# Row maxima of two tiles taken by one VectorE instruction where their banks are neighbours

## Chip, core and metric

One core of one Trainium2 chip. The metric is device time of one execution in microseconds; the change is judged by the median of several executions against that of the kernel before.

## What is computed

A batch of eight images of 32x32 positions and 192 channels goes through an attention block and then a Fourier mixing block, each behind a group normalisation and with a residual:

```python
x = x + attention(group_norm(x), w_qkv, w_o)      # 12 heads of 16, 1024 tokens
x = x + fourier(group_norm(x), w1, b1, w2, b2, bias_w, bias_b)
# attention, per image and head:
attn = softmax((q @ k.T) * 16 ** -0.5)            # 1024 x 1024
out  = (attn @ v) @ w_o
# fourier, per image: y = irfft2(mix2(relu(mix1(rfft2(x))))) + x @ bias_w.T + bias_b
```

All in 32-bit floats. The softmax needs, for each head and query, the largest score over 1024 keys; the change concerns how that maximum is taken.

## The kernel before

**Bodies and steps.** The work is a pipeline over the eight images: `body(b)` is run for b = 0 to 7, the middle ones in a hardware loop, and has 48 steps (`IN_BODY`), 16 for each of three groups of four heads. A step makes four score tiles of 128 keys by 512 queries (`score_tile`, L1196) into three banks of the on-chip accumulator memory (`scores`), ScalarE takes exponentials of them (`exponentials`, L889), and TensorE multiplies the four tiles of the step before with the values (`pv`, L1249).

**The maxima.** The exponentials need the row maxima first. Eleven steps ahead (`AHEAD`), `max_tile` (L1228) makes the same scores once more, the other way round, 128 queries by 512 keys, four tiles i = 0 to 3 a step: tiles 0 and 1 are the odd and even head of a pair over the first 512 keys, tiles 2 and 3 over the second. VectorE's `take_max` (L986) reduces each to one column of `row_max` and counts `max_taken` up. After eight steps `full_max` joins the two halves of the keys (L993), TensorE turns it (`turn_shift`, L1236), VectorE splits it (L999, L1002), and SyncE sends it by four transfers into two rows of `q_stack` (`shifts`).

**The ring.** The tiles of the maxima share four banks (`ring`, `RING` = 4) with all other products, the pieces of the normalisation, projection and Fourier stages: prep pieces (turn, mean, var, qk, v) of the next image, post pieces (proj, turn, mean, var, spread, dftw, dfth, lin, mix1, mix2, idfth, idftw) of the one before. `PREP_AT` and `POST_AT` say at which step a piece stands, ahead of tile 0 (`START`) or behind the output products (`MID`). `ring_order` writes entries one after another, 268 a body, and an entry's bank is its number modulo 4 (`RING_NO`). Before it writes an entry, TensorE waits until the entry that last held the bank has been read (`bank_free`, `bank_held`): the one four before it, or, where a body leaves pieces out, the last that was made in this bank. Body 0 has no post pieces, only four small set-up stages in the places of proj; body 7 has no prep pieces.

**TensorE's order in a step** is fixed by hand: START pieces, tile 0, score 0, tile 1, score 1, the output products, MID pieces, score 2, tile 2, score 3, tile 3. VectorE takes the START pieces, tiles 0 and 1, the MID pieces, tiles 2 and 3.

**Facts of the ring order that the prediction uses.** In 74 of the 96 pairs (tiles 0 and 1, tiles 2 and 3) of a body the two banks are neighbours, in 22 the first is bank 3 and the second bank 0. An entry whose bank was held by the first tile of such a neighbouring pair, with nothing but tile 3 and pieces between: tile 1 of a step, held by tile 2 of the step before, at 21 steps, with one START piece between (lin at 1 and 29, turn 2 and 13, proj 8, 9 and 10, qk 16, 18, 21 and 23, var 20, dftw 25 and 26, dfth 31 and 33, mix1 39, mix2 41 and 42, v 44 and 45); tile 0, held likewise, at 9 steps, with two between (5: idftw, turn; 11: var, proj; 14: turned, turn; 17: qk, qk; 22: turned, qk; 28: qk, lin; 35: mix1, mix1; 37: qk, mix1; 47: idfth, idfth). "turned" is the product of `turn_shift`. In the start-up the tiles of the last 11 steps of the order are made without the pieces; there the banks of the pairs run 23, 30, 23, 12, 01, 30, 23, 01, 30, 12, 01, 30, 23, 12, 01, 23, 12, 30, 23, 23, 23, 01.

Of the kernel before, what the change touches and what calls it, by code (L numbers as in the profile page):

```python
# [8 lines left out]
ALU = mybir.AluOpType  # L9
ACT = mybir.ActivationFunctionType  # L10
AX = mybir.AxisListType
F32 = mybir.dt.float32
# [5 lines left out]
NT = TOK // P  # L18
# [4 lines left out]
STEPS = 16  # L23
# [10 lines left out]
TILES = GH * STEPS  # L34
VW = HD + 2
HMAX = GH * NT // 2
TURN_AT = 4
HUNITS = STEPS // 2
SCORE_BANKS, RING = 3, 4
AHEAD = STEPS // 2 + 3  # L40
# [84 lines left out]
IN_BODY = NG * STEPS  # L125
# [47 lines left out]
RING_NO = {entry: n for n, entry in enumerate(RING_ORDER)}  # L173
# [71 lines left out]
def build(nc, consts, x, w_qkv, w_o, w1, b1, w2, b2, bias_w, bias_b, out):  # L245
# [3 lines left out]
    with ctx:  # L249
        def sb(name, shape, dt=F32):  # L250
            return ctx.enter_context(nc.sbuf_tensor(name, shape, dt))

        def bank(name, n=1):
            return ctx.enter_context(nc.psum_tensor(name, [P, n, HALF], F32))

        def sem(name):
            return ctx.enter_context(nc.semaphore(name))
# [29 lines left out]
        row_max = sb("row_max", [P, 2, HMAX])  # L287
        full_max = sb("full_max", [P, HMAX])
        shift = sb("shift", [HMAX, 2, P], F32R)
# [40 lines left out]
        ring = bank("ring", RING)  # L330
# [29 lines left out]
        max_made = sem("max_made")  # L360
        max_taken = sem("max_taken")
# [19 lines left out]
        def after(eng, s, count):  # L381

            if not isinstance(count, int) or count > 0:
                eng.wait_ge(s, count)
# [54 lines left out]
        def ring_bank(entry):  # L439
            return ring[:, RING_NO[entry] % RING, :]  # L440
# [55 lines left out]
        def max_unit(unit, i):  # L496

            half, m = divmod(unit, HUNITS)
            hp, qt = divmod(m, NT // 2)
            return half, hp, qt, 1 - i % 2, i // 2  # L500

        def max_bank(g, unit, i):

            return ring_bank(("max", (STEPS * g + unit - AHEAD) % IN_BODY, i))

        def turned_in(b, u):
            return ring_bank(("turned", u))[0:HMAX, 0:P]
# [1 line left out]
        def halves(b, g, half):  # L509

            return 2 * NG * b + 2 * g + half
# [51 lines left out]
        def _(sp):  # L563
# [34 lines left out]
            def shifts(b, g, half):  # L598
                after(sp, shift_split, 2 * halves(b, g, half) + 2)
                for n, odd in itertools.product(range(2), range(2)):  # L600
                    row = 64 * odd + KQ + n
                    sp.dma_start(q_stack[row:row + 1, g, half, :, :].bitcast(F32),
                                 shift[HMAX // 2 * odd:HMAX // 2 * (odd + 1), n, :].bitcast(F32)
                                 ).then_inc(shift_in, 16)

            def sums_down(slot):
# [65 lines left out]
            def prologue():  # L672
# [30 lines left out]
                for g in range(NG):  # L703
                    for part_of in ("q0", "k", "q1"):
                        stack(0, g, part_of)
                    if g == 1:
                        shifts(0, 0, 0)

            def body(b, prep, post):
                first = isinstance(b, int) and b == 0  # L710
                for u in range(IN_BODY):
# [21 lines left out]
                    if u in shift_steps(prep):  # L733
                        shifts(*next_half(b, u))
# [242 lines left out]
        def _(dve):  # L977
            def take_max(slot, g, unit, i):
                half, hp, qt, odd, which = max_unit(unit, i)
                no = 4 * unit + i  # L980
                m = HMAX // 2 * odd + NT // 2 * hp + qt
                dve.wait_ge(max_made, TILES * slot + no + 1)
                if unit % HUNITS == 0 and i == 0:

                    after(dve, max_joined, 2 * slot + half)
                nc.vector.tensor_reduce(row_max[:, which, m:m + 1],  # L986
                                        max_bank(g, unit, i),
                                        AX.X, ALU.max).then_inc(max_taken, 1)
                if unit % HUNITS == HUNITS - 1 and i == 3:

                    dve.wait_ge(max_taken, TILES * slot + no + 1)
                    after(dve, shift_turned, 2 * slot + half)
                    nc.vector.tensor_tensor(full_max[:, :], row_max[:, 0, :], row_max[:, 1, :],  # L993
                                            ALU.max).then_inc(max_joined, 1)
# [122 lines left out]
            def prologue():  # L1117
                nc.vector.memset(k_stack[:, :, :].bitcast(F32), 1.0).then_inc(stack_ones, 1)
                nc.vector.memset(xt1[CH:CH + 1, 0, :], 1.0).then_inc(ones_set, 1)
                nc.vector.memset(spec_a[CH:CH + 1, :], 1.0).then_inc(ones_set, 1)  # L1120
                for u in range(IN_BODY):
                    for kind, k in in_order({u: PREP_AT.get(u, NO_PIECES)}):
                        prep_piece(0, kind, k, early_bank(PREP_NO[kind, k]))
                    for kind, k in PREP_FOLLOW.get(u, []):
                        follow(0, 0, kind, k)
                for unit in range(AHEAD):
                    for i in range(4):
                        take_max(0, 0, unit, i)
                    if unit == HUNITS:
                        split_shift(0, 0, 0, turned_in(0, IN_BODY - 3))  # L1130

            def body(b, prep, post):
                first = isinstance(b, int) and b == 0
                for u in range(IN_BODY):
# [7 lines left out]
                    for tile in tiles[:2]:  # L1142
                        take_max(tile[0], *tile[2:])
# [4 lines left out]
                    for tile in tiles[2:]:  # L1148
                        take_max(tile[0], *tile[2:])
# [34 lines left out]
        def _(pe):  # L1184
# [33 lines left out]
            def max_tile(body, u, slot, b, g, unit, i):  # L1218
                half, hp, qt, odd, which = max_unit(unit, i)
                no = 4 * unit + i  # L1220
                if unit == 0 and i == 0:
                    pe.wait_ge(stacked[g], STACK_INCS * (b + 1))
                if unit == HUNITS and i == 0:
                    pe.wait_ge(stacked_second[g], SECOND_INCS * (b + 1))

                bank_free(body, ("max", u, i))
                rows = slice(64 * odd, 64 * odd + KQ)
                mm(max_bank(g, unit, i),  # L1228
                   q_stack[rows, g, half, hp, P * qt:P * (qt + 1)],
                   k_stack[rows, 2 * g + hp, HALF * which:HALF * (which + 1)],  # L1230
                   start=True, stop=True).then_inc(max_made, 1)
# [326 lines left out]
```

## Time and profile before

| | us |
|---|---|
| median of 3 runs | 1567.48 (1566.85 to 1567.92) |
| the profiled execution | 1570.3 |
| its span, first to last instruction | 1568.5 |
| TensorE busy | 1490.9 |
| VectorE busy, of it row maxima | 1221.5, 970.3 |
| ScalarE busy | 1005.6 |

The profile is of one execution. Its page gives, for each engine, the time in which instructions are drawn, and then a chain of waits: from the last instruction back, at each point to what released it. TensorE overlaps instructions, so its busy time is no measure of how full it is. Row groups name the instruction, its result and its operand by the kernel's own names, with the line of the kernel before.

### The profile page before, as it was taken

How to read it: one execution, taken by the hardware profiler on the slowest of the kernel's cores; microseconds unless marked ns; L12 is line 12 of the kernel's file. 1: busy time of each engine (PE TensorE's matmuls, PEld its weight loads, DVE VectorE, ACT ScalarE, POOL GpSimd, SP SyncE). 2: the span in 40 equal slices, each digit the busy share in tenths (PEclk: the TensorE clock that was granted, in tenths of full speed). 3: DMA queues.
4: the chain of work that ended last, by engine and by line, in shares of the span. 5: the costliest groups of instructions: out<-in, count | busy, mean ns of one | idle time of the engine just before them, and what ended most of it. 6: DMA issues, size and time to landing. Idle time of an engine off the chain costs nothing.

```text
span 1568.5 us, 28858 instructions
## 1 busy us (share of the span) xinstructions
PE 1490.9 (95%) x8768; PEld 692.1 (44%) x8768; DVE 1221.5 (78%) x2175; ACT 1005.6 (64%) x1945; POOL 166.8 (11%) x257
## 2 busy tenths in 40 slices
PE   7799999999999999999999999999999999999886
PEld 5333334444444444444444453444544444433454
DVE  4888879987798868988599877988699877887031
ACT  2167766777667666767567776777767776767511
POOL 2000001200003000120013000030002100030000
PEclk9599999999999999999999999999999999989999
DMA  5420223143253232333250431532331432411223
GB/s 116 79 50 18 34 49 69 30 74 59 44 110 51 49 75 55 68 69 64 52 110 15 79 70 24 110 52 48 78 72 28 68 68 44 89 28 31 43 48 83
DMA packets 93892, 94.14 MB, mean 60 GB/s; under 512 B 23201, under 2 KB 75170, under 8 KB 93730
## 3 DMA queue, kind: packets, MB, share of 16 engines
q1 hardware_dynamic: 93730, 92.14, 30.0%
q8 instruction: 82, 1.34, 0.4%
q14 instruction: 80, 0.66, 0.1%
HBM read 14.23 MB, written 6.29 MB: 13 GB/s over the span
## 4 chain that ended last, share of the span: by engine, by line
PE 74%; DVE 13%; issue 4%; SPq 3%; DMA 2%; POOL 1%; ACT 1%; DVEq 0%; POOLq 0%
PE o_acc L1249 20%; PE scores L1196 14%; PE ring L1228 13%; DVE row_max L986 10%; PE ring L1272 6%; PE ring L1318 4%; PE ring L1285 2%; PE ring L1385 2%; PE ring L1372 2%; PE ring L1378 2%; PE ring L1294 1%; PE ring L1364 1%; PE ring L1391 1%; PE ring L1260 1%; SPq L628 1%
## 5 line engine op out<-in xcount | busy, mean ns | idle before, releaser
L986 DVE TENSOR_REDUCE row_max<-ring 128x1 f32<-128x512 f32 x1536 | 970.3, 681 | 165.1 <-PE ring L1228 162.3
L889 ACT ACTIVATE probs<-scores 128x512 f32<-128x512 f32 x1536 | 828.7, 598 | 297.8 <-PE scores L1196 292.2
L1228 PE MATMUL ring<-k_stack,q_stack 48*128 48x512 f32 x1536 | 577.2, 461 | 20.6 <-DVE row_max L986 18.1
L1196 PE MATMUL scores<-q_stack,k_stack 50*128 50x512 f32 x1536 | 578.5, 456 | 3.6 <-DMA q_stack<-shift 2.2
L1249 PE MATMUL o_acc<-probs,v_aug 128*18 128x512 f32 x3072 | 409.9, 606 | 2.3 <-ACT probs L889 1.2
L1196 PEld LDWEIGHTS scores<-q_stack,k_stack 50*128 50x128 f32 x1536 | 239.3, 186 | 297.7 <-ACT probs L889 265.2
L1228 PEld LDWEIGHTS ring<-k_stack,q_stack 48*128 48x128 f32 x1536 | 241.0, 189 | 150.6 <-DVE row_max L986 84.6
L545 POOL TENSOR_TENSOR inv_all<-o_raw,inv_all 128x1024 f32<-128x1024 f32 x23 | 54.2, 2357 | 646.2 <-DVE inv_all L1013 646.2
L1249 PEld LDWEIGHTS o_acc<-probs,v_aug 128*18 128x18 f32 x3072 | 51.8, 96 | 128.1 <-issue 87.8
L1318 PE MATMUL ring<-xt,w_qk 96*128 96x256 f32 x336 | 91.8, 399 | 2.3 <-DVE row_max L986 2.2
L1318 PEld LDWEIGHTS ring<-xt,w_qk 96*128 96x128 f32 x336 | 57.6, 189 | 34.0 <-DVE row_max L986 20.9
L1070 DVE TENSOR_TENSOR x<-ring,x 128x384 f32<-128x384 f32 x28 | 15.5, 554 | 52.0 <-PE ring L1285 52.0
L1051 DVE TENSOR_TENSOR qk_parts<-ring,qk_parts 128x256 fp32r<-128x256 f32 x84 | 34.7, 417 | 21.1 <-ACT qk_parts L919 20.4
L919 ACT CAST qk_parts<-ring 128x256 fp32r<-128x256 f32 x84 | 31.3, 372 | 30.5 <-PE ring L1318 29.7
L1272 PE MATMUL ring<-wo,o_t 96*128 96x192 f32 x248 | 48.1, 338 | 0.9 <-DVE tok_n L1082 0.9
L905 ACT COPY xt<-ring 96x512 f32<-96x512 f32 x28 | 16.2, 582 | 45.8 <-PE ring L1260 45.8
L934 ACT COPY rows_a<-ring 128x384 f32<-128x384 f32 x62 | 29.8, 481 | 23.9 <-PE ring L1391 18.0
L1272 PEld LDWEIGHTS ring<-wo,o_t 96*128 96x128 f32 x248 | 39.6, 190 | 10.2 <-DVE row_max L986 4.5
L1285 PE MATMUL ring<-bias_t,xt 97*128 97x192 f32 x224 | 44.0, 339 | 0.0
L1272 PE MATMUL ring<-wv,xt 96*128 96x192 f32 x224 | 43.9, 339 | 0.0
L1025 DVE BATCH_NORM_STATS2 stats<-xt 96x6 f32<-96x512 f32 x64 | 42.9, 678 | 0.5 <-ACT xt L929 0.5
L1272 PEld LDWEIGHTS ring<-wv,xt 96*128 96x128 f32 x224 | 35.6, 189 | 17.0 <-DVE row_max L986 12.3
(163 smaller groups left out, 1039.8 us busy)
## 6 DMA issues: line engine op xcount, KB each, us to landing
q_stack<-qk_parts SPq DMA_DIRECT2D x288, 64.0 KB, 2.8
k_stack<-qk_parts SPq DMA_DIRECT2D x144, 128.0 KB, 4.4
rows_b<-rows_a SPq DMA_DIRECT2D x128, 96.0 KB, 3.0
spec_b<-spec_a SPq DMA_DIRECT2D x64, 102.0 KB, 2.3
x_in<-in_x_dram SPq DMA_DIRECT2D x8, 768.0 KB, 6.5
x_res<-in_x_dram SPq DMA_DIRECT2D x8, 768.0 KB, 6.8
o_t<-inv_all SPq DMA_DIRECT2D x96, 64.0 KB, 2.3
rows_b<-spec_b SPq DMA_DIRECT2D x32, 192.0 KB, 3.2
```

Source lines behind the costliest of these rows:

```text
L545: ops.tensor_tensor(inv_all[:, :], o_raw[:, :], inv_all[:, :], ALU.mult).then_inc(o_normed, 1)
L889: nc.scalar.activation(probs[:, GH * (s % 2) + h, :], scores[:, n % SCORE_BANKS, :], ACT.Exp, scale=SCALE).then_inc(probs_made, 1)
L986: nc.vector.tensor_reduce(row_max[:, which, m:m + 1], max_bank(g, unit, i), AX.X, ALU.max).then_inc(max_taken, 1)
L1025: nc.vector.bn_stats(stats[:, which, c, half, :], what[0:CH, c, HALF * half:HALF * (half + 1)]).then_inc(stats_done[which], 1)
L1051: nc.vector.tensor_tensor(qk_parts[:, 1, k // 4, cols], bank_[:, 0:QUARTER], qk_parts[:, 0, k // 4, cols].bitcast(F32), ALU.subtract).then ...
L1196: mm(scores[:, n % SCORE_BANKS, :], k_stack[rows, 2 * g + hp, P * kt:P * (kt + 1)], q_stack[rows, g, half, hp, :], start=True, stop=True). ...
L1228: mm(max_bank(g, unit, i), q_stack[rows, g, half, hp, P * qt:P * (qt + 1)], k_stack[rows, 2 * g + hp, HALF * which:HALF * (which + 1)], st ...
L1249: last = mm(o_acc[32 * h:32 * h + VW, 0, :], v_aug[:, g, kt, h, :], probs[:, GH * (s % 2) + h, :], start=(kt == 0), stop=(kt == NT - 1), s ...
L1272: last = mm(bank_[:, C * n:C * (n + 1)], lhs[:, c, P * t:P * (t + 1)], rhs[:, c, :], start=(n == 0 and c == 0), stop=(c == 1), skip_group_ ...
L1285: last = mm(bank_[:, C * n:C * (n + 1)], xt1[rows, c, P * t:P * (t + 1)], bias_t[rows, c, :], start=(n == 0 and c == 0), stop=(c == 1), sk ...
L1318: last = mm(bank_[:, 0:QUARTER], w_qk[:, c, P * (k // 4):P * (k // 4 + 1)], xt[:, c, QUARTER * (k % 4):QUARTER * (k % 4 + 1)], start=(c == ...
L1372: last = mm(bank_[0:CH, P * n:P * n + f.shape[1]], rows_b[:, j, CH * chunk:CH * (chunk + 1)], f, start=True, stop=True)
```

## The change

`take_max` compares the bank numbers of tiles i and i | 1. Where the second is the first plus one, tile 0 (or 2) waits for both tiles, and one `tensor_reduce` over two banks, 2 x 512 elements, gives two columns of `row_max` and counts `max_taken` up by two; tile 1 (or 3) keeps a wait and has no instruction. Where the ring turns over between the two (bank 3, then 0), each keeps an instruction. The two columns are eight apart and stand with the odd head first, so the halves of `shift` that are sent to the rows of `q_stack` are exchanged.

```diff
--- before.py
+++ after.py
@@ -501,7 +501,10 @@
 
         def max_bank(g, unit, i):
 
-            return ring_bank(("max", (STEPS * g + unit - AHEAD) % IN_BODY, i))
+            return ring[:, max_bank_no(g, unit, i), :]
+
+        def max_bank_no(g, unit, i):
+            return RING_NO["max", (STEPS * g + unit - AHEAD) % IN_BODY, i] % RING
 
         def turned_in(b, u):
             return ring_bank(("turned", u))[0:HMAX, 0:P]
@@ -600,7 +603,7 @@
                 for n, odd in itertools.product(range(2), range(2)):
                     row = 64 * odd + KQ + n
                     sp.dma_start(q_stack[row:row + 1, g, half, :, :].bitcast(F32),
-                                 shift[HMAX // 2 * odd:HMAX // 2 * (odd + 1), n, :].bitcast(F32)
+                                 shift[HMAX // 2 * (1 - odd):HMAX // 2 * (2 - odd), n, :].bitcast(F32)
                                  ).then_inc(shift_in, 16)
 
             def sums_down(slot):
@@ -978,14 +981,21 @@
             def take_max(slot, g, unit, i):
                 half, hp, qt, odd, which = max_unit(unit, i)
                 no = 4 * unit + i
-                m = HMAX // 2 * odd + NT // 2 * hp + qt
-                dve.wait_ge(max_made, TILES * slot + no + 1)
+                m = NT // 2 * hp + qt
+                first, second = max_bank_no(g, unit, i), max_bank_no(g, unit, i | 1)
+                paired = second == first + 1
+                dve.wait_ge(max_made, TILES * slot + no + 1 + (paired and i % 2 == 0))
                 if unit % HUNITS == 0 and i == 0:
 
                     after(dve, max_joined, 2 * slot + half)
-                nc.vector.tensor_reduce(row_max[:, which, m:m + 1],
-                                        max_bank(g, unit, i),
-                                        AX.X, ALU.max).then_inc(max_taken, 1)
+                if i % 2 == 0 and paired:
+                    nc.vector.tensor_reduce(row_max[:, which, m::HMAX // 2],
+                                            ring[:, first:first + 2, :],
+                                            AX.X, ALU.max).then_inc(max_taken, 2)
+                elif max_bank_no(g, unit, i & 2) + 1 != max_bank_no(g, unit, i | 1):
+                    m += HMAX // 2 * (1 - odd)
+                    nc.vector.tensor_reduce(row_max[:, which, m:m + 1], ring[:, first, :],
+                                            AX.X, ALU.max).then_inc(max_taken, 1)
                 if unit % HUNITS == HUNITS - 1 and i == 3:
 
                     dve.wait_ge(max_taken, TILES * slot + no + 1)
```

Counted over the program, 592 merged and 352 single reductions take the place of 1536.

**VectorE, steps 31 to 34, as the program has them the first time that they are there in full**, where the pieces of the transform along the height (dfth) are. Before:

```order
L986 TENSOR_REDUCE row_max<-ring 128x1 x8
L1076 COPY spec_a<-ring 96x2x96
L986 TENSOR_REDUCE row_max<-ring 128x1 x2
L1076 COPY spec_a<-ring 96x2x192
L986 TENSOR_REDUCE row_max<-ring 128x1 x6
L1051 TENSOR_TENSOR qk_parts<-ring,qk_parts 128x256
```

Now:

```order
L997 TENSOR_REDUCE row_max<-ring 128x1 x2
L1086 COPY spec_a<-ring 96x2x96
L992 TENSOR_REDUCE row_max<-ring 128x2
L1086 COPY spec_a<-ring 96x2x192
L992 TENSOR_REDUCE row_max<-ring 128x2 x2
L997 TENSOR_REDUCE row_max<-ring 128x1 x2
L1061 TENSOR_TENSOR qk_parts<-ring,qk_parts 128x256
L992 TENSOR_REDUCE row_max<-ring 128x2 x2
```

The copies are dfth 2 and dfth 4, both of step 32. The two maxima between them, tiles 0 and 1 of step 32, have become one instruction; of the six behind, tiles 2 and 3 of step 32 and tiles 0 and 1 of step 33 have become one each, and tiles 2 and 3 of step 33, in banks 3 and 0, stay two.

**VectorE, start-up**, the maxima of eight steps made ahead of the first score tile. Before:

```order
L1051 TENSOR_TENSOR qk_parts<-scores,qk_parts 128x256 x12
L986 TENSOR_REDUCE row_max<-ring 128x1 x32
L993 TENSOR_TENSOR full_max<-row_max 128x16
L986 TENSOR_REDUCE row_max<-ring 128x1 x4
```

Now:

```order
L1061 TENSOR_TENSOR qk_parts<-scores,qk_parts 128x256 x12
L992 TENSOR_REDUCE row_max<-ring 128x2
L997 TENSOR_REDUCE row_max<-ring 128x1 x2
L992 TENSOR_REDUCE row_max<-ring 128x2 x3
L997 TENSOR_REDUCE row_max<-ring 128x1 x2
L992 TENSOR_REDUCE row_max<-ring 128x2 x2
L997 TENSOR_REDUCE row_max<-ring 128x1 x2
L992 TENSOR_REDUCE row_max<-ring 128x2 x2
L997 TENSOR_REDUCE row_max<-ring 128x1 x2
L992 TENSOR_REDUCE row_max<-ring 128x2 x4
L1003 TENSOR_TENSOR full_max<-row_max 128x16
```

Of these 32 maxima, 24 are merged into 12 instructions.

**TensorE, step 33 of the same body**, in the changed kernel, with waits (its lines are ten higher than before): dfth 5, tile 0, score 0, tile 1, score 1, output products.

```order
L1382 MATMUL ring<-cst,rows_b 96x192 [waits post_by_act]
L1238 MATMUL ring<-k_stack,q_stack 128x512 [waits post_by_dve]
L1206 MATMUL scores<-q_stack,k_stack 128x512 [waits probs_made]
L1238 MATMUL ring<-k_stack,q_stack 128x512 [waits max_taken]
L1206 MATMUL scores<-q_stack,k_stack 128x512 [waits probs_made]
L1259 MATMUL o_acc<-probs,v_aug 18x512 [waits o_out,v_ready,probs_made]
L1259 MATMUL o_acc<-probs,v_aug 18x512 x3
```

Nothing is moved on TensorE; its waits stand where they stood, with the same counts. The second L1238 row, tile 1, is the one that waits for `max_taken`, which tile 2 of step 32 counts up.

## Rows read from the trace of the kernel before

**Rows 1.** The page, busy time of each engine.

```profile
PE 1490.9 (95%) x8768; PEld 692.1 (44%) x8768; DVE 1221.5 (78%) x2175; ACT 1005.6 (64%) x1945; POOL 166.8 (11%) x257
```

**Rows 2.** The page, the chain that ended last, shares by engine and by line.

```profile
PE 74%; DVE 13%; issue 4%; SPq 3%; DMA 2%; POOL 1%; ACT 1%; DVEq 0%; POOLq 0%
PE o_acc L1249 20%; PE scores L1196 14%; PE ring L1228 13%; DVE row_max L986 10%; PE ring L1272 6%; PE ring L1318 4%; PE ring L1285 2%; PE ring L1385 2%; PE ring L1372 2%; PE ring L1378 2%; PE ring L1294 1%; PE ring L1364 1%; PE ring L1391 1%; PE ring L1260 1%; SPq L628 1%
```

**Rows 3.** The chain in order of time, 40 to 68 us: start us, us, what.

```profile
43.14 18.03 DVE row_max L986 x30
```

**Rows 4.** The chain's shares by line, 60 to 240 us, then 240 to 1400 us.

```profile
by line: DVE row_max L986 27.7%; PE o_acc L1249 18.9%; PE ring L1228 13.8%; PE scores L1196 11.1%; issue 4.3%; PE ring L1318 4.1%; PE ring L1272 3.3%; PE ring L1260 2.6%; SPq L628 1.4%; POOL inv_all L545 1.3%; DVE qk_parts L1051 1.2%; SPq L
...
by line: PE o_acc L1249 22.0%; PE scores L1196 15.3%; PE ring L1228 15.1%; DVE row_max L986 7.0%; PE ring L1272 6.7%; issue 4.9%; PE ring L1318 4.8%; PE ring L1285 2.8%; PE ring L1385 2.5%; PE ring L1372 2.4%; PE ring L1378 2.3%; PE ring L1
```

**Rows 5.** The costliest groups, the row maxima: busy us, mean ns, idle before, releaser.

```profile
L986 DVE TENSOR_REDUCE row_max<-ring 128x1 f32<-128x512 f32 x1536 | 970.3, 681 | 165.1 <-PE ring L1228 162.3
```

**Rows 6.** Waits: us in total, times, longest.

```profile
PEld scores L1196 <- ACT probs L889: 265.2, 331, 1.3
...
DVE row_max L986 <- PE ring L1228: 162.3, 280, 6.4
...
PEld ring L1228 <- DVE row_max L986: 84.6, 183, 1.7
```

**Rows 7.** Timeline, 709 to 714.5 us (steps 32 and 33): start us, us, engine.

```profile
709.79 0.73 PE L1228 MATMUL ring<-k_stack,q_stack 48*128 48x512 f32 x2
...
710.37 2.47 DVE L986 TENSOR_REDUCE row_max<-ring 128x1 f32<-128x512 f32 x4
...
710.45 0.57 PE L1372 MATMUL ring<-cst,rows_b 128*96 128x192 f32 x2
...
710.95 0.50 PE L1228 MATMUL ring<-k_stack,q_stack 48*128 48x512 f32 x1
...
711.29 0.40 PE L1228 MATMUL ring<-k_stack,q_stack 48*128 48x512 f32 x1
...
712.62 0.72 PE L1228 MATMUL ring<-k_stack,q_stack 48*128 48x512 f32 x2
...
713.18 1.29 DVE L986 TENSOR_REDUCE row_max<-ring 128x1 f32<-128x512 f32 x2 [0.34 <-PE ring L1228]
```

**Rows 8.** Timeline, 174 to 178 us, in body 0.

```profile
175.53 0.73 PE L1228 MATMUL ring<-k_stack,q_stack 48*128 48x512 f32 x2
...
176.09 2.48 DVE L986 TENSOR_REDUCE row_max<-ring 128x1 f32<-128x512 f32 x4 [0.42 <-PE ring L1228]
176.10 0.39 PE L1228 MATMUL ring<-k_stack,q_stack 48*128 48x512 f32 x1
...
176.84 0.50 PE L1228 MATMUL ring<-k_stack,q_stack 48*128 48x512 f32 x1 [0.35 <-DVE row_max L986]
```

**Rows 9.** VectorE's groups by form: two additions, 384 and 1024 elements.

```profile
L1070 DVE TENSOR_TENSOR x<-ring,x 128x384 f32<-128x384 f32 x28 | 15.5, 554 | 52.0 <-PE ring L1285 52.0
...
L545 DVE TENSOR_TENSOR inv_all<-o_raw,inv_all 128x1024 f32<-128x1024 f32 x1 | 1.2, 1226 | 0.0
```

**Rows 10.** The chain, 780 to 900 us: one piece of each kind.

```profile
785.43 0.84 PE ring L1294 x2
...
796.12 0.21 PE ring L1236
...
802.28 1.50 PE ring L1272 x8
...
817.99 0.57 PE ring L1260 x4
...
838.91 1.06 PE ring L1318 x4
```

**Rows 11.** The chain, 900 to 1010 us: a mix1 and a var piece.

```profile
914.03 0.63 PE ring L1378 x2
...
996.46 0.26 PE ring L1312 x2
```

## Prediction

> **What bounds the kernel now.** I read the page from the top. TensorE is drawn busy 95% of the span, VectorE 78%, ScalarE 64% [rows 1]. The chain of waits is the view that counts: TensorE holds 74% of it and VectorE 13%, of which 10%, some 157 us, are row maxima [rows 2]. So TensorE's own stream is nearly everything, and VectorE decides in patches. By stretch: in the start-up a run of 30 maxima stands in the chain alone, 18.03 us, 0.601 us each [rows 3]; between 60 and 240 us the maxima hold 27.7% of the chain, between 240 and 1400 us 7.0% [rows 4]. VectorE's idle time before a maximum, 165.1 us, is waiting for TensorE [rows 5]; the other way TensorE's weight loads waited 84.6 us for maxima, 183 times [rows 6]. The two hand work back and forth over four banks, so what matters is not how much VectorE works but **when a bank is released**.
>
> The handshake as it is: in the stretch at 712.62 two tiles are made, the second ending at 713.34; VectorE starts on the first at 713.18, before the second is there, and has both in 1.29 us [rows 7]. Ends within such a pair lie 0.24 us apart (710.95+0.50 and 711.29+0.40), so the first ended at 713.10 and VectorE started 0.08 behind it. From a release to the next matrix instruction: the maximum that starts at 176.09 and lasts 0.68 us ends at 176.77, and TensorE starts at 176.84 [rows 5, 8], 0.07 us.
>
> **The cost of the merged instruction.** No row shows a reduction over 1024 elements. One over 512 takes 0.681 us [rows 5]. A VectorE addition takes 0.554 us for 384 and 1.226 us for 1024 elements [rows 9], 1.05 ns an element, so 512 more are 0.54 us: I take **1.22 us**. The ends for it: 1.36 us (two whole ones) and 1.20 us (two at the back-to-back pace of 0.601). Separately the two take 1.29 us [rows 7], so a merged one saves 0.07 us. 74 of the 96 pairs of a body are merged, 592 in all: 41 us less VectorE time, but it counts only where VectorE holds the chain: 157 us there are some 122 pairs of 1.29 us, 77% of them merged, by 0.07 us each: **-7 us**.
>
> Here a rule speaks for the change. The Trainium skill, "VectorE: DVE Perf Modes", section on the TRN2 errata, gives VectorE instructions that read PSUM a fixed 120 cycles of 0.96 GHz each; by that the merged form would save 0.125 us a pair, and the term would be -12 us. [...] The trace does not agree: four maxima of 0.68 us stand in 2.47 us, not 2.72 [rows 7], so part of the fixed cost is already hidden; the measured spacing decides.
>
> **What is added: two waits.** (1) The instruction waits for the second tile. Where VectorE is idle it starts 0.24 us later, so the second bank is free 0.24-0.07 = 0.17 us later. (2) The first bank is released with the second: after the second tile's end 0.07 + 1.22 + 0.07 = **1.36 us** pass before TensorE may write it again. Queued behind that wait on TensorE are the next score tile (so ScalarE) and the four output products; nothing passes them.
>
> Who asks for the first bank that soon? By the ring order, an entry takes the bank of the entry four before. Tile 1 of a step takes that of tile 2 of the step before when one piece lies between; there are 21 such places a body. Tile 0 does so when two lie between, 9 places. All others have the output products, or a whole pair and pieces, between. Worked on step 33 [rows 7]: tile 3 of step 32 ends at 709.79+0.73 = 710.52; the piece starts at 710.45 and tile 0 at 710.95; tile 1 starts at 711.29, because tile 2 was released at 710.37+0.68 = 711.05. Merged: 710.52 + 1.36 = 711.88, **0.59 us later**. In general tile 1 comes the piece + 0.27 us behind the end of tile 3, so the wait is 1.09 us less the piece; for tile 0, 0.34 us earlier, 1.43 less both pieces. Lengths of pieces: turn 0.57, v, proj and lin 1.50, qk 1.06, idftw and dftw 0.84, turned 0.21 [rows 10], mix1 0.63, mean and var 0.26 [rows 11]; dfth 5 0.50, from the step just read, and dfth 1 I take as 0.84.
> Tile 1, a body: turn 2 x 0.52, var 0.83, dftw 2 x 0.25, dfth 0.25 and 0.59, mix1 0.46; v, proj and lin nothing, qk and mix2 0.03 at most; 3.7 us. Tile 0: turned+turn 0.65, turned+qk 0.16, mix1+mix1 0.17; 1.0 us. Together **4.7 us a body**, for the six full bodies 1 to 6: **+28 us**. Where VectorE is already behind, TensorE waits up to 1.22-0.68 = 0.54 us longer, but VectorE loses nothing and a part comes back; for the half dozen pieces that follow a step with VectorE work, between nothing and 2.5 us a body, I take 1.2: **+7 us**.
>
> Body 0 has hardly any post pieces, so at most of the 21 places nothing covers. At 175.53 to 176.84 [rows 8]: tile 3, the second of the two from 175.53 on, ends at 176.26; merged, tile 1 starts at 176.26+1.36 = 177.62 against 176.84, 0.78 us later, VectorE idle meanwhile. Eleven places of 0.78 and three half covered by the set-up: **+10 us** (5 to 18). The last body lacks the prep pieces: five places of 0.78 and the rest as above: **+7 us**. In the start-up 17 of 22 pairs are merged; eight of them follow a merged pair that holds one of their banks, and each time VectorE must idle for release, tile and start, 0.07 + 0.5 + 0.07 = 0.64 us, where it ran on before [rows 3]; less 17 x 0.07: **+4 us**.
>
> The swapped rows of the four shift transfers change no size and no count: nothing. The wait left for the second tile is long met: nothing.
>
> **Sum:** 28+7+10+7+4 = 56. About a tenth of the chain is on other engines and queues [rows 2], where TensorE's delay is swallowed: -6. VectorE's gain -7. Total +43 us, 2.7%. The profiled execution took 1570.3 us (span 1568.5); the median of the runs is 1567.5, and the sum is put on that: **1610 us** (for a profiled execution 1613).
>
> **Rivals.**
> - *Faster.* VectorE is the bound more widely than the chain says, and the tiles are made while it is still busy with older ones, so that waiting for the second costs nothing and the 0.07 us count. It decides if VectorE starts the merged instruction over 0.3 us behind the second tile at most places. For it: 10% of the chain. Against: VectorE idles 165.1 us, and starts ahead of the second tile [rows 7, 8]. It gives 1567.5-7 = 1561 us. Chance 0.08. (By the fixed cost that the Trainium skill, "VectorE: DVE Perf Modes", the TRN2 errata, gives, this case would be 1556 us.)
> - *Nothing comes through.* TensorE would wait at these places anyway, for ScalarE: weight loads of score tiles wait 265.2 us for it [rows 6]. Against: TensorE's own idle time is at most 5% of the span [rows 1], and ScalarE is fed by the same delayed tiles. Near 1569 us, chance 0.06.
> - *The merged read runs at two whole ones, 1.36 us.* Then each covered place costs 0.14 us more, some 12 a body in six and 25 in the rest: +14, and VectorE's -7 turns to +7: 1610+28 = 1638 us. Chance 0.08.
> - *Slower, but half.* The delays at the places overlap with VectorE's lag: 14+4+5+4+4 = 31, less 3 swallowed and 7 gained, +21: 1589 us. Chance 0.2; the forecast has 0.58.
>
> **Range and chances.** From below the half case with its own doubt, from above the slow read with body 0 at its upper end (+8): 1577 to 1645 us. A measurement can tell about 0.2%, 3 us, from no change. Faster 0.08, within 0.2% 0.06, slower 0.86.
>
> **What would show it.** Reductions of 128x1024 last 1.2 us, 592 of them, and 352 of the old kind; VectorE's busy time falls by 30 to 45 us while its idle time before maxima rises well past 165 us; TensorE waits for row maxima over 150 us in weight loads; in step 33 tile 1 starts 0.9 us behind tile 0, not 0.34; between 240 and 1400 us the maxima's share of the chain is above 7.0%. A share of the chain that fell, with the same gaps between tiles, would make me wrong.

## The result and the profile after

| | before | changed |
|---|---|---|
| median, us | 1567.48 | 1679.27 |
| runs, us | 1566.85 to 1567.92 | 1679.23 to 1696.26 |
| profiled execution, us | 1570.3 | 1679.27 |
| its span, us | 1568.5 | 1677.4 |
| granted TensorE clock of the span | 0.975 | 0.966 |

The ratio is **1.074 (95% interval 1.069 to 1.080)**: 112 us slower, where 43 were forecast and the range ended at +78. The waits that were forecast came, at the places that were named; the loss was sized at less than half. In every ratio here a run over 1.5% above the fastest of its kernel is left out, which concerns one run, the 1615.5 us of `wait_only` below.

The page after, busy times and the groups of the maxima (busy us, mean ns, then the engine's idle time before them and who ended it), against [rows 1, 5]:

```profile
PE 1524.9 (91%) x8768; PEld 706.3 (42%) x8768; DVE 1203.7 (72%) x1583; ACT 1011.9 (60%) x1945; POOL 165.8 (10%) x257
...
L992 DVE TENSOR_REDUCE row_max<-ring 128x2 f32<-128x1024 f32 x592 | 721.0, 1223 | 241.6 <-PE ring L1238 236.5
L1238 PE MATMUL ring<-k_stack,q_stack 48*128 48x512 f32 x1536 | 599.4, 468 | 83.3 <-DVE row_max L992 76.2
...
L1238 PEld LDWEIGHTS ring<-k_stack,q_stack 48*128 48x128 f32 x1536 | 247.0, 189 | 241.1 <-DVE row_max L992 143.4
L997 DVE TENSOR_REDUCE row_max<-ring 128x1 f32<-128x512 f32 x352 | 226.3, 682 | 50.0 <-PE ring L1238 48.5
```

The merged instruction takes 1.223 us, as forecast, 592 times; VectorE's busy time falls by 18 us only, where 30 to 45 were forecast. The 768 pairs of before took 970.3/768 = 1.263 us each, since maxima that follow each other in fours overlap more than the 1.29 us of a lone pair; merging saves 0.04 us a pair, not 0.07. Its idle time before maxima goes from 165.1 to 291.6 us (241.6 + 50.0). The Trainium skill, "VectorE: DVE Perf Modes", the TRN2 errata, gives 120 cycles plus one per element at 0.96 GHz: 1.19 us for this one and 0.66 for the single; the rows say 1.223 and 0.682, within 4%. That two single ones overlap is seen in the rows: 1.29 us for both, 0.07 less than twice 0.682.

The waits after (us in total, times, longest), against [rows 6]:

```profile
PEld scores L1206 <- ACT probs L892: 258.5, 325, 0.9
DVE row_max L992 <- PE ring L1238: 236.5, 361, 6.6
...
PEld ring L1238 <- DVE row_max L992: 143.4, 232, 2.0
...
PE ring L1238 <- DVE row_max L992: 76.2, 121, 1.4
...
PEld ring L1238 <- DVE row_max L997: 33.2, 72, 1.1
```

TensorE's weight loads wait 176.6 us for maxima (143.4 + 33.2) instead of 84.6, and its multiplications 76.2 us for merged ones, where they waited 18.1 us for maxima before. The waits of score tiles for ScalarE have hardly moved, 258.5 against 265.2, so this view shows nothing that was swallowed there. (The chain of waits of this profile can be followed back only into body 7, its shares add up to some 14%, so it isn't read.)

Step 33, the place that the prediction worked out [rows 7], in the changed kernel's timeline:

```profile
775.11 0.40 PE L1238 MATMUL ring<-k_stack,q_stack 48*128 48x512 f32 x1
...
775.65 1.23 DVE L992 TENSOR_REDUCE row_max<-ring 128x2 f32<-128x1024 f32 x1 [0.21 <-PE ring L1238]
...
775.94 0.49 PE L1238 MATMUL ring<-k_stack,q_stack 48*128 48x512 f32 x1
...
776.93 0.18 PEld L1238 LDWEIGHTS ring<-k_stack,q_stack 48*128 48x128 f32 x1 [0.81 <-DVE row_max L992]
776.93 0.49 PE L1238 MATMUL ring<-k_stack,q_stack 48*128 48x512 f32 x1 [0.49 <-DVE row_max L992]
...
777.01 0.49 PE L1206 MATMUL scores<-q_stack,k_stack 50*128 50x512 f32 x1
...
777.43 1.05 PE L1259 MATMUL o_acc<-probs,v_aug 128*18 128x512 f32 x8
777.52 1.23 DVE L992 TENSOR_REDUCE row_max<-ring 128x2 f32<-128x1024 f32 x1 [0.65 <-PE ring L1238]
...
778.42 0.73 PE L1238 MATMUL ring<-k_stack,q_stack 48*128 48x512 f32 x2
```

Tile 3 of step 32 ends at 775.11+0.40 = 775.51, VectorE starts at 775.65, ends at 776.88, and tile 1 starts at 776.93, 0.99 us behind tile 0 where it was 0.34. That is 0.65 us more; 0.59 were forecast, with VectorE's start 0.07 us behind the tile instead of the 0.14 seen. But look further: from tile 1 to tile 2 of the same step it is 778.42-776.93 = 1.49 us; before it was 712.62-711.29 = 1.33 [rows 7]. **The step lost another 0.16 us behind the wait.** Two rows of the kernel before, which [rows 7] leave out, show what stood otherwise:

```profile
710.95 0.73 PE L1196 MATMUL scores<-q_stack,k_stack 50*128 50x512 f32 x2
...
711.10 0.18 PEld L1228 LDWEIGHTS ring<-k_stack,q_stack 48*128 48x128 f32 x1
```

There the weights of tile 1 were loaded from 711.10 on, 0.19 us ahead of it, and the second score tile of the row, score 1, ran beside it (it ended at 710.95+0.73 = 711.68, tile 1 at 711.69). In the changed kernel the weights come with tile 1, at 776.93, and score 1 at 777.01, 0.08 us behind it. The loss was in no term.

The place in body 0 [rows 8]:

```profile
197.56 0.73 PE L1238 MATMUL ring<-k_stack,q_stack 48*128 48x512 f32 x2
...
198.13 0.40 PE L1238 MATMUL ring<-k_stack,q_stack 48*128 48x512 f32 x1
...
198.46 1.23 DVE L992 TENSOR_REDUCE row_max<-ring 128x2 f32<-128x1024 f32 x1 [0.48 <-PE ring L1238]
...
199.74 0.49 PE L1238 MATMUL ring<-k_stack,q_stack 48*128 48x512 f32 x1 [1.21 <-DVE row_max L992]
```

From the second tile's end, 197.56+0.73 = 198.29, to tile 1 at 199.74 it is 1.45 us, and VectorE, which before ran four maxima in 2.48 us here, has one instruction and then idles. Tile 1 starts 1.61 us behind tile 0 (198.13), where it was 0.74 [rows 8].

Where the time went, in stretches that end at the same tile in both kernels (start to the first tile of body 0; body 0; bodies 1 to 6; body 7 to its last tile; the rest). Columns: stretch, length, busy time and count of TensorE, weight loads, VectorE, ScalarE, POOL, then the granted TensorE clock, DMA share and GB/s. Before:

```profile
0.00:71.50 71.50, 53.09 (x173) 31.41 (x173) 45.05 (x72) 10.28 (x22) 9.86 (x35) 0.76 0.46 93
71.50:234.50 163.00, 152.00 (x909) 61.97 (x908) 137.26 (x245) 113.78 (x217) 8.35 (x14) 0.97 0.24 42
234.50:1311.00 1076.50, 1056.83 (x6462) 489.25 (x6463) 898.57 (x1613) 751.51 (x1457) 128.38 (x180) 0.99 0.32 62
1311.00:1440.40 129.40, 124.06 (x742) 50.93 (x738) 111.28 (x193) 87.59 (x166) 15.38 (x17) 0.96 0.23 49
1440.40:1568.50 128.10, 104.90 (x495) 58.49 (x491) 29.39 (x54) 42.43 (x85) 4.81 (x11) 0.96 0.25 55
```

After:

```profile
0.00:76.70 76.70, 48.94 (x173) 28.40 (x173) 44.95 (x55) 10.28 (x22) 9.86 (x35) 0.76 0.44 90
76.70:267.50 190.80, 164.00 (x909) 65.33 (x908) 135.51 (x171) 114.70 (x217) 8.35 (x14) 0.90 0.20 35
267.50:1414.80 1147.30, 1087.57 (x6462) 504.15 (x6462) 884.25 (x1169) 756.56 (x1457) 127.52 (x180) 0.99 0.31 58
1414.80:1548.70 133.90, 119.39 (x740) 50.02 (x740) 109.34 (x136) 87.94 (x166) 15.24 (x17) 1.00 0.22 47
1548.70:1677.40 128.70, 104.99 (x495) 58.37 (x491) 29.61 (x53) 42.42 (x85) 4.81 (x11) 0.96 0.25 55
```

| stretch | before | after | difference | forecast |
|---|---|---|---|---|
| start-up | 71.5 | 76.7 | +5.2 | +4 |
| body 0 | 163.0 | 190.8 | +27.8 | +10 |
| bodies 1 to 6 | 1076.5 | 1147.3 | +70.8 | +35 |
| body 7 | 129.4 | 133.9 | +4.5 | +7 |
| tail | 128.1 | 128.7 | +0.6 | 0 |
| swallowed, VectorE's gain | | | 0 | -13 |

In body 0 something else has changed: the granted clock fell from 0.97 to 0.90 (the engine runs at 2.4 or, half granted, 1.2 GHz).

The traces also let one compare step by step, from tile 0 of a step to tile 0 of the next. In the six full bodies the clock was full in both kernels in 280 of the 288 steps; these grew by 64.7 us, the other eight by 6.1. In body 0 it was full in both in 38 of the 48 steps; these grew by 12.2 us, the other ten by 15.6.

### The profile page after: what moved, and what is told of

It is laid out like the page before. It is cut to its first block and busy times, and to the rows that moved or that the text cites. A ratio compares the mean times of both kernels' runs of the same rounds, so it can differ in the third digit from the quotient of the medians.

```text
span 1677.4 us, 28660 instructions
## 1 busy us (share of the span) xinstructions
PE 1524.9 (91%) x8768; PEld 706.3 (42%) x8768; DVE 1203.7 (72%) x1583; ACT 1011.9 (60%) x1945; POOL 165.8 (10%) x257
## 5 line engine op out<-in xcount | busy, mean ns | idle before, releaser
L992 DVE TENSOR_REDUCE row_max<-ring 128x2 f32<-128x1024 f32 x592 | 721.0, 1223 | 241.6 <-PE ring L1238 236.5
L1238 PE MATMUL ring<-k_stack,q_stack 48*128 48x512 f32 x1536 | 599.4, 468 | 83.3 <-DVE row_max L992 76.2
L1206 PE MATMUL scores<-q_stack,k_stack 50*128 50x512 f32 x1536 | 600.0, 463 | 1.4 <-ACT probs L892 1.4
L1259 PE MATMUL o_acc<-probs,v_aug 128*18 128x512 f32 x3072 | 416.2, 614 | 1.4 <-ACT probs L892 1.2
L1206 PEld LDWEIGHTS scores<-q_stack,k_stack 50*128 50x128 f32 x1536 | 244.9, 187 | 297.0 <-ACT probs L892 258.5
L1238 PEld LDWEIGHTS ring<-k_stack,q_stack 48*128 48x128 f32 x1536 | 247.0, 189 | 241.1 <-DVE row_max L992 143.4
L997 DVE TENSOR_REDUCE row_max<-ring 128x1 f32<-128x512 f32 x352 | 226.3, 682 | 50.0 <-PE ring L1238 48.5
L1295 PEld LDWEIGHTS ring<-bias_t,xt 97*128 97x128 f32 x224 | 38.3, 199 | 14.8 <-issue 9.8
```

Of the source, the lines that this page charges most:

```text
L992: nc.vector.tensor_reduce(row_max[:, which, m::HMAX // 2], ring[:, first:first + 2, :], AX.X, ALU.max).then_inc(max_taken, 2)
L997: nc.vector.tensor_reduce(row_max[:, which, m:m + 1], ring[:, first, :], AX.X, ALU.max).then_inc(max_taken, 1)
L1206: mm(scores[:, n % SCORE_BANKS, :], k_stack[rows, 2 * g + hp, P * kt:P * (kt + 1)], q_stack[rows, g, half, hp, :], start=True, stop=True). ...
L1238: mm(max_bank(g, unit, i), q_stack[rows, g, half, hp, P * qt:P * (qt + 1)], k_stack[rows, 2 * g + hp, HALF * which:HALF * (which + 1)], st ...
L1259: last = mm(o_acc[32 * h:32 * h + VW, 0, :], v_aug[:, g, kt, h, :], probs[:, GH * (s % 2) + h, :], start=(kt == 0), stop=(kt == NT - 1), s ...
L1295: last = mm(bank_[:, C * n:C * (n + 1)], xt1[rows, c, P * t:P * (t + 1)], bias_t[rows, c, :], start=(n == 0 and c == 0), stop=(c == 1), sk ...
```

## Experiments

A remark on the clock first. Runs of the kernel before took 1565.7 us at a granted clock of 0.977, 1575.1 at 0.970 and 1585.3 at 0.962: some 13 us for each 0.01. The runs of one kernel lie 8 to 25 us apart, so each result is given with the clock of its runs, and where a few us matter the six full bodies are compared by windows, where the clock is 0.98 or 0.99 in all, and by the steps in which it was full in both kernels.

### The two waits apart

`wait_only` keeps the wait for both tiles and nothing else; `release_only` the common release; `both_apart` both, but without merging. Of the edits here and below only the lines that matter are shown; those of the changed kernel keep the swapped halves of `shift`.

```diff
 wait_only: the wait for the second tile stays, then for every tile
+nc.vector.tensor_reduce(row_max[:, which, m:m + 1], ring[:, first, :],
+                        AX.X, ALU.max).then_inc(max_taken, 1)
 release_only
-dve.wait_ge(max_made, TILES * slot + no + 1 + (paired and i % 2 == 0))
+dve.wait_ge(max_made, TILES * slot + no + 1)
 release_only and both_apart: two instructions, counted up with the second
+one = nc.vector.tensor_reduce(row_max[:, which, m:m + 1], ring[:, first, :], AX.X, ALU.max)
+if not merged:
+    one.then_inc(max_taken, 1)
+elif i % 2 == 1:
+    one.then_inc(max_taken, 2)
```

> Both maxima of a neighbouring pair stay instructions of their own with releases of their own; only the wait for the second tile before the first maximum is kept. Theory A (late release of the first bank): the start shifts by at most 0.24 us and each bank is free that much later, so TensorE is rarely reached: 1580 to 1590 us (+12 to +22). Theory B (waiting for the second tile empties VectorE's lead): most of the 112 us are here, 1640 us or more.

> Two instructions, the first starts as soon as its tile is there, but both banks are released with the second (the count goes up by two behind it). Theory A: the first bank is free 0.61 us later, and this is most of the loss: 1645 to 1665 us (+78 to +98). Theory B: near the kernel before, 1570 to 1590 us.

> The wait for the second tile and the common release, but with two instructions of 0.68 us. Against the changed kernel it lacks only the merging itself, 0.07 us a pair on VectorE. Theory A: the release of both banks is 0.07 us later than merged at every place that waits, some 20 a body: 1679 plus 8 to 15, 1687 to 1694 us. If the merging saves nothing on the path: 1679.

| | median us | ratio (95%) | clocks of the runs |
|---|---|---|---|
| wait_only | 1589.9 | 1.011 (1.004 to 1.018) | 0.964 to 0.980 |
| release_only | 1625.9 | 1.038 (1.030 to 1.046) | 0.961 to 0.977 |
| both_apart | 1693.7 | 1.076 (1.068 to 1.085) | 0.946 to 0.958 |

The six full bodies (1076.5 us before, 1147.3 after) in `wait_only`, `release_only` and `both_apart`, same columns as above:

```profile
247.60:1342.80 1095.20, 1071.45 (x6461) 497.19 (x6462) 903.14 (x1612) 752.51 (x1455) 128.52 (x180) 0.98 0.32 61
```

```profile
250.30:1363.60 1113.30, 1070.34 (x6461) 497.72 (x6462) 903.68 (x1612) 756.06 (x1457) 128.62 (x180) 0.99 0.31 60
```

```profile
296.10:1437.60 1141.50, 1082.91 (x6463) 502.72 (x6462) 910.29 (x1612) 756.11 (x1457) 127.51 (x180) 0.99 0.31 59
```

The late release (theory A) is the larger part, +36.8 us in these bodies against +18.7 for the wait; in the steps with a full clock it is 37.0 against 10.1, so of the 18.7 much is clock. Theory B (the wait empties VectorE's lead, so that most of the loss is in `wait_only`) falls. But theory A had most of the loss in `release_only`, 1645 to 1665 us, and it took 1625.9: the two waits together cost +65.0, in the steps with a full clock 64.1, and so 17 us more than the sum of each alone. Step 33 shows how: from tile 0 to tile 1 it is 0.34 us before, 0.39 in `wait_only`, 0.75 in `release_only` and 0.99 in `both_apart`. The first 0.2 us of a delay are there within the slack of the place, and the second delay then counts in full.

`both_apart` is not slower than the change in these bodies (1141.5 against 1147.3), where the expectation had +8 to +15 for the whole run. So **merging itself gained nothing**. Of the 5.8 us by which it is even ahead, 4.3 lie in the eight steps where the clock was half in one of the two or in both, 1.6 in the 280 others. In full runs `both_apart` is slower, and hits the number that was expected, only by its lower clock, 0.95 against 0.966: body 0 alone takes 24.5 us longer, at a clock of 0.74.

`wait_only` shows the cost behind a wait by itself, at step 33 in its timeline:

```profile
732.37 0.49 PE L1233 MATMUL ring<-k_stack,q_stack 48*128 48x512 f32 x1
...
732.76 0.50 PE L1233 MATMUL ring<-k_stack,q_stack 48*128 48x512 f32 x1
...
734.25 0.73 PE L1233 MATMUL ring<-k_stack,q_stack 48*128 48x512 f32 x2
```

Tile 1 is only 0.05 us late (0.39 for 0.34), yet tile 2 follows 1.49 us later instead of 1.33. This short delay costs the same 0.16 us behind it as the 0.65 us of the change.

### Which pairs

`places_only` merges the 30 pairs at the places of the prediction, `others_only` the other 44. A second line, not shown, gives every pair that isn't merged its two instructions, here and in the selections below.

```diff
-paired = second == first + 1
+u = (STEPS * g + unit - AHEAD) % IN_BODY
+at_place = i >= 2 and u in (0, 1, 4, 7, 8, 9, 10, 12, 13, 15, 16, 17, 19, 20, 21, 22, 24, 25,
+                            27, 28, 30, 32, 34, 36, 38, 40, 41, 43, 44, 46)
+paired = second == first + 1 and at_place        # others_only: not at_place
```

> Only the 30 pairs (tiles 2 and 3) are merged whose first bank is asked for by tile 0 or tile 1 of the next step with only pieces between; the other 44 stay apart. Theory A with the places as named in the prediction: two thirds of the loss, 1630 to 1650 us. Rival C (each merged pair costs about the same, 112/592 us): 30 of 74, 1613 us. The prediction's own sum for these places was 28+10+7 and part of 4: 1610 us.

> The 30 pairs of places_only stay apart, the other 44 are merged. places_only cost 81 us, the change 112. If the two halves add up (theory A with two kinds of place: tiles 0 and 1, and START pieces whose bank a late VectorE holds): +31, 1595 to 1605 us. The prediction allowed 7 us for these: 1575 us. If these 44 hurt only together with the others: 1565 to 1575 us. Every 0.01 of granted clock is worth some 13 us in the runs of the kernel before (1565.7 at 0.977, 1585.3 at 0.962), so runs of about 0.975 are compared.

`places_only`: 1648.2 us, ratio 1.050 (1.042 to 1.059), clock 0.968 to 0.978. `others_only`: 1600.8 us, 1.023 (1.018 to 1.028), 0.965 to 0.976. The six full bodies of each:

```profile
249.50:1377.50 1128.00, 1079.38 (x6463) 498.92 (x6463) 896.80 (x1433) 755.92 (x1457) 127.60 (x180) 0.99 0.31 59
```

```profile
242.30:1336.30 1094.00, 1062.25 (x6463) 490.85 (x6462) 888.92 (x1349) 753.26 (x1456) 128.63 (x180) 0.99 0.32 61
```

+51.5 and +17.5, together 69.0 of the 70.8: the two halves add up, and the places carry three quarters, so rival C (each merged pair costs alike) falls. In the steps with a full clock it is 51.1 and 16.2. The prediction had 28 and 7 for them. Of the 2.9 us a body that `others_only` loses, 2.2 lie between tile 3 of a step and tile 0 of the next, where the START pieces stand. Tile by tile against the kernel before, the places of `places_only` grew by 0.57 and 0.58 us (turn), 0.84 (var), 0.30 twice (dftw), 0.32 and 0.65 (dfth), 0.52 (mix1), 0.08 to 0.25 at the six with qk and mix2, and 0.43, 0.41, 0.40 and 0.21 for tile 0: 6.2 us a body against the 4.7 worked out. Behind twelve of them the way from tile 1 to tile 2 grew by 0.12 to 0.19 each, 2.1 us a body. The 0.3 that are left of the 8.6 aren't assigned.

### Which bodies

`early_only` merges in the start-up and body 0, `late_only` from body 1 on.

```diff
-paired = second == first + 1
+early = isinstance(slot, int) and STEPS * slot + unit < IN_BODY + AHEAD
+paired = second == first + 1 and early            # late_only: not early
```

> Merged from body 1 on; start-up and body 0 stay apart. In the trace the changed kernel is 33 us behind at the end of body 0. If that part stands by itself: 1679-33 = 1646 us. If half of it comes from the clock, which is lower there (0.5 of full speed for 48 us from 43 us on, against 38 before, and four more dips up to 235 us), the granted clock of the run rises from 0.966 to 0.975.

> The complement: merged in the start-up and body 0 alone, 91 of the 592 pairs. By the trace +33: 1600 us, with a granted clock near 0.966. By pairs alone (112 x 91/592): 1585 us. By the prediction (10+4): 1581 us.

`late_only`: 1655.5 us, 1.054 (1.048 to 1.060), clock 0.960 to 0.974; its two runs at 0.973 and 0.974 took 1645.0 and 1648.2, near the 1646 that was expected; the clock of all its runs did not rise to the 0.975 that the other case had. `early_only`: 1604.3 us, 1.025 (1.020 to 1.029), 0.961 to 0.972; its run at 0.972 took 1594.3. So in full runs the early merged pairs, a sixth of all, cost between 29 and 39 us. The traces part the two exactly. The six full bodies in `late_only`, then in `early_only`:

```profile
234.00:1382.10 1148.10, 1089.51 (x6463) 506.03 (x6462) 884.31 (x1169) 756.09 (x1457) 127.69 (x180) 0.99 0.31 58
```

```profile
263.80:1340.50 1076.70, 1056.42 (x6462) 489.78 (x6462) 898.64 (x1613) 751.50 (x1457) 128.40 (x180) 0.99 0.32 62
```

They are as long as in the change (1147.3) and as before (1076.5), and begin at 234.0 us (234.5 before) and at 263.8 (29.3 later): neither part acts on the other. The trace's reading (+33) stands, the share by pairs (1585) and the prediction's (1581) don't.

How much of body 0 is clock? Body 0 in `early_only`, in the kernel of the next section and in `both_apart`; the two waits are in all three:

```profile
76.80:263.80 187.00, 159.84 (x907) 64.38 (x906) 135.42 (x171) 114.73 (x217) 8.36 (x14) 0.93 0.20 36
```

```profile
79.00:279.10 200.10, 179.06 (x909) 72.10 (x908) 135.53 (x171) 113.36 (x217) 8.36 (x14) 0.84 0.19 33
```

```profile
80.80:296.10 215.30, 191.72 (x909) 74.97 (x908) 140.13 (x245) 115.49 (x217) 8.34 (x14) 0.74 0.17 31
```

With the change's own row above: 187.0 us at a clock of 0.93, 190.8 at 0.90, 200.1 at 0.84, 215.3 at 0.74, close to 1.5 us for each 0.01. At the 0.97 of the kernel before that line gives about 181. `chosen_pairs` (below), which merges nothing in body 0, had a lower clock there in its trace too, and took 2.6 us more than the kernel before, 0.9 us for each 0.01:

```profile
71.80:237.40 165.60, 155.86 (x909) 62.99 (x908) 137.37 (x245) 113.65 (x217) 8.35 (x14) 0.94 0.23 42
```

So of the 27.8 us some 6 to 10 are clock and 18 to 22 waits. This is read from runs of kernels that differ a little; a run with the waits and a held clock wasn't made, so the split is an estimate. Why the clock falls isn't shown: all four kernels with the two waits have less than before, from 0.93 to 0.74, but `chosen_pairs` has 0.94 without them.

### Score 1 ahead of the waiting tile

```diff
 for tile in tiles[0:1]:
     max_tile(b, u, *tile)
 score_tile(b, g, s, 0)
+score_tile(b, g, s, 1)
 for tile in tiles[1:2]:
     max_tile(b, u, *tile)
-score_tile(b, g, s, 1)
```

in the changed kernel (`after_score1_first`) and in the kernel before (`before_score1_first`); `before_score0_first` puts score 0 ahead of tile 0 instead.

> The changed kernel with TensorE's order in the first half of a step changed from tile 0, score 0, tile 1, score 1 to tile 0, score 0, score 1, tile 1. A waiting tile 1 then holds up only the output products. Theory A with a restart cost (score 1 behind the wait loses its place beside tile 1, 0.1 to 0.2 us at some 14 places a body): 12 to 22 us faster than the changed kernel at the same clock, 1657 to 1667 us. If the wait alone counts: 1679 us; if tile 1, now made later, costs VectorE more: slower.

> The same order in the kernel before. TensorE waits there at fewer places (weight loads 84.6 us for maxima, against 177 in the changed kernel), so half as much: 1560 to 1567 us. It would be slower, 1570 to 1590 us, if the two tiles of a step lie further apart and VectorE runs dry between them.

> The kernel before with the first half of a step in the order of the second: score 0, tile 0, score 1, tile 1. ScalarE gets its tile some 0.1 us sooner, VectorE its own later. If ScalarE's wait for scores (292 us) reached the end, 1555 to 1563 us; if the maxima's do, 1568 to 1580 us; I expect no difference, 1564 to 1570 us.

`after_score1_first` took 1694.6 us (ratio to the kernel before 1.084, 1.079 to 1.088), slower than the change, against what was expected; its clock was 0.935 to 0.954. Step 33 in its timeline:

```profile
789.73 0.49 PE L1238 MATMUL ring<-k_stack,q_stack 48*128 48x512 f32 x1
...
789.73 0.73 PE L1206 MATMUL scores<-q_stack,k_stack 50*128 50x512 f32 x2
...
790.72 0.49 PE L1238 MATMUL ring<-k_stack,q_stack 48*128 48x512 f32 x1 [0.26 <-DVE row_max L992]
...
791.14 1.05 PE L1259 MATMUL o_acc<-probs,v_aug 128*18 128x512 f32 x8
...
792.13 0.73 PE L1238 MATMUL ring<-k_stack,q_stack 48*128 48x512 f32 x2
```

The wait is as long (0.99 us behind tile 0), and from tile 1 to tile 2 it is now 1.41 us, neither 1.49 nor 1.33 (without a wait it is 1.33 in this order too, in `before_score1_first`): half of the cost behind the wait is score 1's place, the other half is not. That the other half is the weights, loaded only with the waiting tile, fits the rows but wasn't tried by itself. That is worth 1 us a body at the twelve places, where the expectation had 12 to 22 us in all, and the lower clock elsewhere took more than it gave: body 0 is 9.3 us longer than in the change (200.1 at a clock of 0.84), body 7 is 9.0 us longer (142.9 at 0.89, against 133.9 at 1.00), the six full bodies are 3.5 us shorter (1143.8). The expectation was right on the sign at the steps, and wrong on the size and on the run.

`before_score1_first`: 1565.8 us, 1.000 (0.997 to 1.003). `before_score0_first`: 1564.0 us, 0.998 (0.996 to 1.000). The second is at the edge of what can be told; no version here clearly beats the kernel before.

### One place, and pairs without a place

```diff
 one_place
+paired = second == first + 1 and (i >= 2 and u == 19)
 chosen_pairs
+paired = second == first + 1 and (not early and i < 2 and u in (4, 20, 22, 32, 34, 36, 38, 46))
```

> One pair a body is merged, tiles 2 and 3 of step 19, whose first bank tile 1 of step 20 asks for behind the short var piece; eight merged instructions in all. The prediction's sum for this place is 0.83 us a body, 6.6 us: 1572 us. In the changed kernel the step from tile 0 to tile 1 of step 20 grew by 0.84 us. If a stall of TensorE costs more than its wait (weights loaded late, the next score tile no longer beside), it is 1.0 us a body or more, 8 us. If such a delay is caught up by a lead elsewhere, under 3 us.

> Merged only at tiles 0 and 1 of eight steps from body 1 on, where in the trace of before VectorE starts at least as late as the second tile is there and the first bank's next entry comes over 0.1 us behind the merged end. Each saves VectorE 0.07 us and should cost nothing: between -4 us and 0, 1563 to 1568 us. If merging hurts by itself, it shows here as +3 or more.

`one_place`: 1577.8 us, 1.0064 (1.0046 to 1.0083), +7 to +13 us for eight instructions. Tile by tile, step 20 grew by 0.84 us in each body, as worked out, and the way to tile 2 not at all: TensorE had waited at this place before (0.39 us from tile 0 to tile 1, not 0.34), so the cost behind a wait was already paid. Eight bodies of 0.84 are 6.7 of the 10 us. In the six full bodies 0.84 each would be 5.0; they grew by some 7.5, of which 4.8 are in the steps with a full clock in both kernels and 2.8 in the six others. So this delay on TensorE comes through whole; it isn't caught up, and the rest is clock.

`chosen_pairs`: 1567.5 us, 1.0009 (0.9984 to 1.0034), -2.5 to +5.3 us. Merged where neither wait costs anything, the instruction neither helps nor hurts; the 4 us of VectorE time that it saves don't arrive, they lie outside the interval. The swapped halves of `shift` are in this kernel too, and so cost nothing beyond that interval.

## Why the prediction was wrong

**Right.** The way: the merged instruction's length (1.22), the release of the first bank with the second, the places by the ring order, the wait there (0.59 forecast, 0.65 measured at step 33; 0.83 and 0.84 at step 20; 0.78 and 0.87 in body 0, 1.61 us from tile 0 to tile 1 where it was 0.74). Of the signs in the profile, 592 and 352 instructions, idle time of VectorE up, weight loads waiting over 150 us and tile 1 0.99 us behind tile 0 came. VectorE's busy time fell by 18 us and not by 30 to 45, and the chain's share between 240 and 1400 us can't be read. That it is slower was forecast.

**Wrong, by terms of the sum:**
1. *"Tile 1, a body: ... 3.7 us. Tile 0: ... 1.0 us"* (+28): 8.6 us a body, +51.5. This is the step that failed first: the sum priced a stall of TensorE at its length alone. Behind each new one another 0.12 to 0.19 us go, 2.1 us a body; half of that because the next score tile, else beside the waiting tile, comes after it. The waits themselves came to 6.2 us a body: from the second tile's end it was 1.42 us (0.14 to VectorE's start, 1.23, 0.05 to TensorE's) and not 1.36, which at 18 places makes 1 us. The cost behind a wait was to be had: in the trace of before, from tile 1 to the output products it is 0.33 us (median) in some 290 steps where tile 1 came straight behind tile 0, and 0.43 in some 80 where it had waited.
2. *"Where VectorE is already behind ... a part comes back, I take 1.2"* (+7): 2.9 us a body, +17.5, above the 15 of the upper bound. That a part comes back is not borne out: `one_place` shows a delay passing whole.
3. *"Body 0 ... +10"*: +27.8. Some 18 to 22 are waits (the upper bound was 18), and 6 to 10 the granted clock, which stood in no term; the sum assumed the clock of before.
4. *"About a tenth of the chain ... where TensorE's delay is swallowed: -6"* and *"VectorE's gain -7"*: neither came. `both_apart` against the change and `chosen_pairs` show no gain of merging; the chain's 10% for maxima was not time that a shorter maximum gives back.
5. The last body (+7 for +4.5) and the start-up (+4 for +5.2) were near.

Every term but that of the last body erred to the same side; the doubts of the second were settled by halving, and two deductions were taken. With the upper bounds that the text itself gave and no deduction it is 28+15+18+7+4 = 72 us; with 2.1 us a body for starting again, 1 for the longer wait (19 in all) and at most 10 for the clock, 101. Of the rivals, "slower, but half" got the chance that belonged to a case on the other side, delays that add up whole and take the clock along.

## What to carry to other kernels

Before two reads of a small ring of buffers are merged, ask when the first buffer is written again: merging holds it for the whole second read and for the second's arrival, and where the producer comes back within that time it stalled here by the difference, whole, at every turn. The saving is one instruction's overhead less what back-to-back instructions overlap anyway (here 0.07 us of 0.68), and it counts only where that engine really sets the pace. Add to each new stall of TensorE the cost of starting again, and read the granted clock of each stretch beside its time.

## What the runs showed of the hardware

- Two reductions of 512 elements take 1.29 us, one of 2 x 512 takes 1.223 us: 0.07 us saved, half of the 0.14 us by which it is shorter than two single ones of 0.682 end to end.
- A TensorE stall costs 0.12 to 0.19 us beyond its length where TensorE did not wait before, 0.16 even where it delays the tile by 0.05 us only; half of it disappears where the other matrix product stands ahead of the waiting one.
- Of kernels whose body 0 has the same work and the same waits, the granted clock in that stretch was between 0.74 and 0.93, and 0.01 of it was worth 1.5 us of 190. With the work and waits of the kernel before it was 0.97 or 0.94.
